# Building slot tables on one core: comparisons merged on VectorE, half of the bucket one-hots moved off GpSimd, slot one-hots scaled by GpSimd

## The reference, cut to what matters

```
h = relu(layernorm(x));  x = x + hypergraph_conv(relu(hypergraph_conv(h, W1, b1)), W2, b2)
    hypergraph_conv: xt = h @ W;  e = B_inv * segment_sum(xt[src], dst)
                     out = D_inv * segment_sum(e[dst], src) + b
h = relu(layernorm(x));  x = x + message_layer(h, src, dst, edge_weight)
    message_layer: e = silu(silu([h[src], h[dst], w] @ eW1 + eb1) @ eW2 + eb2)
                   agg = segment_sum(e, src);  out = silu([h, agg] @ nW1 + nb1) @ nW2 + nb2
```

## Time and profile before

| | us |
|---|---|
| median of 3 runs | 8857.22 (8846.52 to 8869.2) |
| profiled execution, its own time | 8864.02 |
| its span | 8862.3 |
| granted TensorE clock, mean | 0.956 |

### The profile page before, as it was taken

The page is one execution under the profiler, slowest core; times in us unless marked ns, Lnnn a source line. Parts: engine busy times, 40 slices in busy tenths (PEclk is TensorE's granted clock), DMA queues, the critical chain, the costliest instruction groups (busy, mean ns, idle before and its releaser), DMA issues. The chain is left out here.

```text
span 8862.3 us, 258190 instructions
## 1 busy us (share of the span) xinstructions
PE 7877.5 (89%) x80997; PEld 7191.2 (81%) x80997; DVE 7406.3 (84%) x20481; ACT 5157.5 (58%) x14322; POOL 2812.5 (32%) x4182
## 2 busy tenths in 40 slices
PE   2989998999989988999888899869999999999997
PEld 2777777777777778999788888759998999999995
DVE  7999999999999995777688888548888888888884
ACT  3777777777777770000577788425555555555553
POOL 4977778777777750000000000001111111111110
PEclk9999999999999999999799999759999999999998
DMA  2767667766676677666699999643333333333333
GB/s 71 158 152 157 154 153 157 155 155 153 156 156 153 156 159 199 190 191 170 148 223 222 214 245 245 139 142 109 104 106 106 103 106 106 105 104 105 107 104 74
DMA packets 1523049, 1310.03 MB, mean 148 GB/s; under 512 B 797344, under 2 KB 1337364, under 8 KB 1521212
## 3 DMA queue, kind: packets, MB, share of 16 engines
q1 hardware_dynamic: 1506126, 1269.86, 58.6%
q0 software_dynamic: 14112, 26.84, 1.2%
q10 hardware_dynamic: 1840, 0.53, 0.0%
HBM read 777.89 MB, written 361.62 MB: 129 GB/s over the span
## 5 line engine op out<-in xcount | busy, mean ns | idle before, releaser
L662 POOL TENSOR_SCALAR OH<-iot,kd 128x102 bf16<-128x102 bf16 x3440 | 2285.3, 683 | 3.5 <-PE S L799 3.5
L2257 POOL DMA_INDIRECT Qx<-tab_q,tidx x294 | 320.9, 1091 | 4904.5 <-DVE skt L2291 2584.5
L1478 PE MATMUL wp<-AF,XS 128*128 128x256 f32 x9604 | 1196.3, 283 | 167.6 <-issue 123.4
L841 PE MATMUL HP<-T3a,RB 128*128 128x193 bf16 x9604 | 1209.2, 249 | 124.3 <-ACT RB L965 124.3
L1478 PEld LDWEIGHTS wp<-AF,XS 128*128 128x128 f32 x9604 | 1148.5, 191 | 198.4 <-issue 198.3
L1504 ACT ACTIVATE AF<-RG 128x1536 fp32r<-128x1536 uint8 x686 | 1022.9, 1491 | 332.6 <-PE wp L1478 226.0
L965 ACT ACTIVATE RB<-PS 128x256 int16<-128x256 f32 x2401 | 895.6, 379 | 520.2 <-PE PS L826 479.2
L2278 ACT ACTIVATE Z<-Zb 128x512 f32<-128x512 f32 x882 | 556.1, 630 | 994.3 <-DVE Zb L2335 948.8
L841 PEld LDWEIGHTS HP<-T3a,RB 128*128 128x128 fp8e4 x9604 | 858.8, 98 | 249.1 <-issue 160.8
L926 ACT ACTIVATE LH<-LB,pl 128x64 f32<-128x64 bf16 (+8 forms) x4116 | 1008.4, 330 | 0.0
L2335 DVE TENSOR_TENSOR Zb<-p,eb2s 128x512 f32<-128x512 f32 x882 | 609.3, 691 | 450.1 <-PE p L2228 276.9
(11 more groups left out here) (344 smaller groups left out, 15460.4 us busy)
## 6 DMA issues: line engine op xcount, KB each, us to landing
RG<-adjT SPq DMA_DIRECT2D x1372, 224.0 KB, 6.6
sdb<-bk SPq DMA_DIRECT2D x245, 768.0 KB
adj<-RB SPq DMA_DIRECT2D x343, 448.0 KB, 2.8
adjT<-RT SPq DMA_DIRECT2D x686, 224.0 KB, 3.8
RG<-adj SPq DMA_DIRECT2D x686, 224.0 KB, 4.5
sdb<-bk SPq DMA_DIRECT2D x49, 384.0 KB
WR<-wk SPq DMA_DIRECT2D x882, 9.0 KB
tab_p<-Pst SPq DMA_DIRECT2D x25, 512.0 KB, 3.0
```

The lines of the kernel that those rows point to most:

```text
L662: ins = e.tensor_scalar(OH[:, g * GT + k, :], iot1[:, 0:KEYS], kd[:, g * GT + k:g * GT + k + 1], None, ALU.is_equal)
L841: ins = e.matmul(HP[:, h * W3:(h + 1) * W3], lhsT=pair[:, x_, h * P:(h + 1) * P], rhs=T3a[:, 2 * (u - 1) + x_, :], start=False, stop=True, ...
L1478: ins = e.matmul(ps[b][:, 0:256], lhsT=XS[:, n * PB + m, :, :].rearrange("p c f -> p (c f)"), rhs=AF[:, (b + n) % 3, m, :], start=n == 0 a ...
```

## The change

What it does:

1. **Counting.** The odd list is no longer packed as 256 * count. `OA` holds even and odd source one-hots of two units (512 elements, one instruction), `OB` is gone; `OD` of two units is one instruction of 1024 elements. TensorE writes even and odd counts side by side (512 columns), and ScalarE's `keep` reads 512 values and writes 512 bytes. `counted` is one instruction instead of five.
2. **Bucket one-hots.** VectorE makes those of the first `DT` = 3 tiles of a group in one instruction (`match`), three groups ahead; GpSimd makes the other two.
3. **Ranks.** VectorE adds neighbouring one-hots (`plus`, tile `SP`), and TensorE uses three matmuls of 306, 204 and 102 columns in place of four of 408, 306, 204 and 102.
4. **Slot one-hots.** VectorE compares all five tiles in one instruction (`LB`, 5 by the group's greatest width). ScalarE scales one tile (`AT` = 1), GpSimd the other four in one instruction (`scaled`).
5. GpSimd makes the next chunk's `kd` and `pl` at slot `KEY_AT` = 8 of the turn before, in two buffers.

```diff
-AT = 3
+AT = 1
+DT = 3
+AHEAD = 3
+KEY_AT = 8
...
 GpSimd
-                            for k in range(GT):
-                                ins = e.tensor_scalar(OH[:, g * GT + k, :], iot1[:, 0:KEYS], kd[:, g * GT + k:g * GT + k + 1], None, ALU.is_equal)
+                            for k in range(DT, GT):
+                                ins = e.tensor_scalar(OH[:, g * GT + k, :], iot1[:, 0:KEYS], kd[b][:, g * GT + k:g * GT + k + 1], None, ALU.is_equal)
                             ins.then_inc(v_oh, 1)
+                        def scaled(i, b, g):
+                            after(v_lb, i * NGR + (g + 1))
+                            after(p_s, i * NGR + (g - 1))
...
+                            e.tensor_tensor(LH[g % 2][:, AT:GT, :, 0:w], LB[g % 2][:, AT:GT, 0:w].unsqueeze(2).to_broadcast([P, n, 2, w]),
+                                            pl[b][:, :, t + AT:t + GT].rearrange("p c t -> p t c").unsqueeze(3).to_broadcast([P, n, 2, w]),
+                                            ALU.mult).then_inc(v_lh, 1)
...
 TensorE, ranks
+                            e.wait_ge(v_rk, added(v))
-                            for k in range(GT - 1):
-                                m = GT - 1 - k
-                                ins = e.matmul(b[:, (k + 1) * KEYS:GT * KEYS], lhsT=ones[:, :], rhs=w[:, k:k + 1, :].to_broadcast([P, m, KEYS]), ...
+                            e.matmul(tiles[:, 2:GT, :], lhsT=ones[:, :], rhs=SP[g % 2][:, 0:1, :].to_broadcast([P, GT - 2, KEYS]), ...
+                            e.matmul(tiles[:, 1:GT:2, :], lhsT=ones[:, :], rhs=w[:, 0:GT - 1:2, :], ...
+                            e.matmul(tiles[:, GT - 1, :], lhsT=ones[:, :], rhs=SP[g % 2][:, 1, :], ...
...
 ScalarE, keep
-                            e.activation(RB[n % NSLOT][:, k, :].bitcast(i16), bank(u)[:, 0:256], ACT.Copy,
-                                         accum_out=gs[:, u:u + 1]).then_inc(a_u, 1)
+                            e.activation(RB[n % NSLOT][:, k, :].bitcast(u8).rearrange("p (n x) -> p n x", x=2),
+                                         bank(u)[:, :].rearrange("p (x n) -> p n x", x=2), ACT.Copy, accum_out=gs[:, u:u + 1]).then_inc(a_u, 1)
...
 VectorE, ranks: behind the reductions now match(i, g + AHEAD, b) and plus(i, g + 2)
+                            e.tensor_tensor(OH[:, t:t + DT, :], iot1[:, 0:KEYS].unsqueeze(1).to_broadcast([P, DT, KEYS]),
+                                            kd[b][:, t:t + DT].unsqueeze(2).to_broadcast([P, DT, KEYS]), ALU.is_equal).then_inc(v_rk, 1)
+                            e.tensor_tensor(SP[g % 2][:, :, :], w[:, :, 0, :], w[:, :, 1, :], ALU.add).then_inc(v_rk, 1)
...
 VectorE, places
-                            for k in range(AT):
-                                ins = e.tensor_scalar(LB[g % 2][:, k, 0:w], by_rank(g, iot1, iotr, w), float(OWN - 1), rk[:, t:t + 1], ALU.add, ALU.is_equal)
-                            for k in range(AT, GT):
-                                ins = e.scalar_tensor_tensor(LH[g % 2][:, k, :, 0:w], ranked..., rk[:, t:t + 1], pl[:, :, t:t + 1]..., ALU.is_equal, ALU.mult)
+                            e.tensor_tensor(LB[g % 2][:, :, 0:w], by_rank(g, GT, w), rk[:, t:t + GT].unsqueeze(2).to_broadcast([P, GT, w]),
+                                            ALU.is_equal).then_inc(v_lb, 1)
...
 VectorE, unit
-                                for y in range(2 if u < NU - 1 else 1):
-                                    e.tensor_scalar(OB[k % PAIRS][:, y, :], iot1[:, 0:P], SBk[:, b:b + 1], 256.0, ALU.is_equal, ALU.mult)
+                                e.tensor_tensor(OA[k % PAIRS][:, 0:2 * n * P]..., (iot4 if n == 2 else iot2)[:, 0:P, :], SBs[:, b:b + 2 * n]..., ALU.is_equal)
+                                e.tensor_tensor(OD[k % PAIRS][:, 0:n, :, :], iot2..., SBd[:, b:b + 2 * n]..., ALU.is_equal).then_inc(v_un, 1)
```

More of the change, by code:

```diff
@@ L497, in gnn_kernel @@
                 LH = [sbt(p1, f"LH{n}", [P, GT, 2, P], fp32) for n in range(2)]
-                LB = [sbt(p1, f"LB{n}", [P, AT, P], bf16) for n in range(2)]
+                LB = [sbt(p1, f"LB{n}", [P, GT, P], bf16) for n in range(2)]
                 OHf = [sbt(p1, f"OHf{n}", [P, GT, KEYS], fp32) for n in range(2)]
@@ L519, in gnn_kernel @@
                 pl = [sbt(p1, f"pl{n}", [P, 2, TC], fp32) for n in range(2)]
-                kd = sbt(p1, "kd", [P, TC], fp32)
+                kd = [sbt(p1, f"kd{n}", [P, TC], fp32) for n in range(2)]
                 ddc = sbt(p1, "ddc", [P, 2], fp32)
@@ L525, in gnn_kernel @@
                 rj = sbt(p1, "rj", [P, KEYS], fp32)
+                SP = [sbt(p1, f"SP{n}", [P, 2, KEYS], bf16) for n in range(2)]
                 cb = [sbt(p1, f"cb{n}", [P, KEYS], bf16) for n in range(2)]
@@ L530, in gnn_kernel @@
                 room = sbt(p1, "room", [P, KEYS], bf16)
-                iotr = sbt(p1, "iotr", [P, P], bf16)
                 iofr = sbt(p1, "iofr", [P, P], fp32)
                 d_ct = sem("c_dct")
-                SBk = sbt(p1, "SBk", [P, 2 * KEYS], fp32)
+                SBk = sbt(p1, "SBk", [P, 4], fp32)
                 Ui = sbt(p1, "Ui", [P, P], bf16)
@@ L592, in wide_at, with seen, added, ranked @@
                     return WIDE[t % HT]
-                def by_rank(g, up, down, w):
-                    return up[:, 0:w] if g < HG else down[:, P - w:P]
+                def seen(v):
+                    return (3 * v - 2 if v >= AHEAD else v + 1) if isinstance(v, int) else v * 3 - 2
+                def added(v):
+                    return max(3 * v + 2, AHEAD + 1) if isinstance(v, int) else v * 3 + 2
+                def ranked(v):
+                    return v * 3 + (2 * AHEAD)
+                def used(t):
+                    w, g = wide_at(t), t // GT
+                    a = 0 if g < HG else wide_at(g * GT + GT - 1) - w
+                    return slice(a, a + w)
+                def by_rank(g, n, w):
+                    v = iofo[:, 0:w] if g < HG else iofr[:, P - w:P]
+                    return v.unsqueeze(1).to_broadcast([P, n, w])
                 def ends_of(v):
@@ L674, in turn @@
                         def turn(i, b, behind):
-                            keys(i)
-                            payload(i, b)
                             for g in range(NGR):
-                                onehots(i, g)
-                                if behind and g == NGR // 2:
-                                    diagonal(i - 2)
+                                if g == KEY_AT:
+                                    keys(i + 1, 1 - b)
+                                    payload(i + 1, 1 - b)
+                                onehots(i, b, g + AHEAD)
+                                scaled(i, b, g)
+                                if behind and g == NGR // 2:
+                                    diagonal(i - 1)
+                        keys(0, 0)
+                        payload(0, 0)
+                        for g in range(AHEAD):
+                            onehots(0, 0, g)
                         turn(0, 0, False)
-                        turn(1, 1, False)
+                        turn(1, 1, True)
                         turn(2, 0, True)
@@ L1080, in unit @@
                                 for q in range(4):
[L1081 to L1082 removed]
+                                    ins = e.tensor_scalar(OZ[:, q, :], iot1[:, :], SBk[:, q:q + 1], None, ALU.is_equal)
                                 ins.then_inc(v_un, 1)
@@ L1180, in _ @@
                         e.wait_ge(c_init, 4)
+                        for g in range(AHEAD):
+                            match(0, g, 0)
+                        plus(0, 0)
+                        plus(0, 1)
                         turn(0, 0, True, False, False, False)
```

138 lines of the change are left out of this document (68 added, 70 removed).

## The result

| | before | after |
|---|---|---|
| median, us | 8856.67 (8846.52 to 8869.2, 4 runs) | 8644.92 (8638.71 to 8657.88, 4 runs) |
| span of the profiled execution | 8862.3 | 8637.0 |
| granted TensorE clock, mean | 0.956 | 0.96 |

The ratio is 0.9762, 95% interval 0.9745 to 0.9779: 2.4% faster. 8675 was predicted, 8460 to 8900 as the range.

A forecast was written before the change was run, and what follows sets the result against it. VectorE was taken to bound building: 51.7 us of work, 2.3 of gaps and 7.0 of port stalls make 61.0 a turn against 64.7. Over 48 turns, plus 5 us for turn 0, that gives 8675 us; range 8460 to 8900.

The forecast's parts named there:

- VectorE bounds the turn: Building: VectorE's instructions set the turn, 62.4 us of work in 64.7, falling to 51.7 of work with the change.
- The merged instructions' rates: VectorE in building: units 23.3 us a turn instead of 31.6, places save 9.0, match adds 5.7, plus adds 2.7.
- The port: Building: GpSimd's products and VectorE's two-tensor instructions exclude each other in SBUF, stalling VectorE 7.0 us a turn.
- the bounds of 2.8 and 12.2: VectorE's stall a turn: 2.8 us if products start during PSUM reads, 12.2 if they always get in between unit instructions.
- The gaps: VectorE's time between instructions in a building turn, 2.3 us, kept unchanged and added to 51.7 for 54.0 us.
- The other engines stay below: Building, per turn: TensorE below 56.1 us, ScalarE 47.8, GpSimd 35.8 before any stall, so none was forecast to bind.
- the change touches building alone: Premise that only the building stage changes, so only its turns were forecast and no gain in the message stage.
- Rival 1: Building: the port costs little and TensorE becomes the bound; turns of 55 to 58 us, 8400 to 8540; chance 0.25.
- Rival 2: Building: stalls past 10.7 us, or slow `keep`, undo the change; turn about 66 us, 8926, or 9200 by `keep`; chance 0.15.
- Rival 3: Building: no effect, stalls of 10 to 11 us give back what merging saves; 8830 to 8880 us; chance 0.08.
- -8.3 -1.8: VectorE's forecast savings a building turn from counting: 8.3 us on units, 1.8 on counted and sorted_.
- -9.0 +5.7 +2.7 +7.0: VectorE's forecast terms a building turn: places save 9.0 us; match adds 5.7, plus 2.7, stalls by GpSimd's products 7.0.

The follow-up runs named there:

- e_vscale: Against the changed kernel: VectorE scales the four tiles itself, in one instruction behind LB, and GpSimd does no product; 8544 us, ratio to before 0.983, turn 63.14 us.
- c_rest: The changed kernel with its counting part undone, so parts 2 to 5 of the change alone; 9003 us, ratio to before 1.020, turn 70.54 us.
- e_split: The changed kernel with each GpSimd product of four tiles split into two products of two tiles; 8469 us, ratio to before 0.976, turn 61.55 us.
- e_at2: The changed kernel with AT = 2: ScalarE scales two tiles of a group, GpSimd three; 8474 us, ratio to before 0.974, turn 61.43 us.
- l_after_msg: The changed kernel with 117 more TensorE semaphore increments, putting the message loop where it stands in the kernel before; 8586 us, ratio to before 0.988.
- b_count_at2: The kernel before with the counting part alone, AT = 2 and 139 more TensorE semaphore increments ahead of the message stage; 8389 us, ratio 0.951, turn 58.11 us.
- c_count: The kernel before with the counting part of the change alone; 8538 us, ratio to before 0.984, turn 61.38 us.

## Why the prediction was right, and where not

The total of 8675 is 30 us off, and that it is so close is luck: 183 us were predicted for building and 103 came; 118 came from the message stage, for which the prediction had nothing. The two errors cancel. What was right without luck is the direction, the bound and most terms of the turn; building alone would have given about 8763, still within the range.

- *VectorE bounds the turn, and still does.* Right: 60.2 of 62.75 us busy.
- *The merged instructions' rates.* Right. By the almost undisturbed means of e_vscale less 0.08 us: units 25 x (0.61 + 0.35) = 24.0 us (23.3 predicted), match 14 x 0.40 = 5.6 (5.7), plus 14 x 0.18 = 2.5 (2.7). VectorE's work without stalls is 52.3 us, 51.7 predicted.
- *The port.* The mechanism is shown (e_vscale). The term was too small: 7.0 predicted, 7.9 of standing still measured, and c_rest (7.7), e_split (6.6) and e_at2 (5.3, with three tiles) are between the bounds of 2.8 and 12.2 as well. That the one value chosen between them, 7.0, came this near is partly chance. What was left out is where the stalls fall: small steps of about 0.2 us take 1.34 (`cinv_d`), 1.29 (`E`) and 0.79 us (`w`) when a product meets them.
- *The gaps.* 2.3 us were carried over from before; after, 62.75 - 60.2 = 2.5. With 0.6 of work, 0.9 of stall and 0.2 of gaps, the turn comes to 62.7.
- *The other engines stay below.* Right: ScalarE 47.0 us (47.8), `keep` 601 ns (620). TensorE is busy 56.5, below 62.75. GpSimd has 43.5 us; 35.8 were predicted before any stall.
- *The step that failed* is the one before all others: "the change touches building alone". It touches building's text alone. Parts 2 to 5 moved everything behind them on TensorE by 117 instructions, and the loop of the message stage lost its gaps. Without that the first comparison would be 8645 + 118 = about 8763, 1.1% faster and not 2.4%. That is a working from the stage's length, and l_after_msg bears it out with 0.988 on chip A, where the stage's difference is 49 us; on chip B it is 60.
- *Rival 1* (the port costs little) fell with e_vscale. *Rival 2's* outcome, slower, is that of parts 2 to 5 taken alone (c_rest, 1.020), but not by its mechanism: the stalls there are 7.7 us, not over 10.7. The counting part paid for it. *Rival 3* (stalls give back just what the merging saves) holds of GpSimd's products by themselves: they bring VectorE 9.8 us and cost 9.4.

The prediction also didn't take the change apart. The sum "-8.3 -1.8" for counting and "-9.0 +5.7 +2.7 +7.0" for the rest stood in it: by it the rest was a loss of 6.4 us for VectorE. The only thing for it was ScalarE's relief, which one tile on VectorE gives more cheaply (b_count_at2).

## What to carry to other kernels

Add the terms up for each part of a change by itself; a part that is a loss can hide behind one that is a gain, and a helper engine can cost the engine that it helps nearly all that it takes off it (9.4 of 9.8 us here). When a stage that nobody edited changes its time, look for `issue` gaps in the middle of one statement inside a loop, and move the loop by some hundred instructions (117 and 139 did it here) before believing any other cause. Compare two versions of a long program stage by stage, or with later loops at the same place.

## What the runs showed of the hardware

- Products on GpSimd stop VectorE whole: a two-element copy took 1342 ns and ended with the product. The Trainium skill, SBUF — State Buffer, section Who interferes with whom, calls the shared pair an exclusive lock held for the whole instruction, and Perfetto Trace Analysis, section Optimizing Scalar/DVE Operations, warns that moving work between the two might not help. The trace agrees, with a balance of 0.35 us a turn.
- It goes the other way as well: GpSimd's one-hots, which have a scalar and one streamed tensor, have means of 687, 765 and 789 ns in before, c_count and b_count_at2, and 852 in e_vscale, where VectorE does the products as well, with a minimum of 525 to 530. So GpSimd waits as well when VectorE has much two-tensor work; no run changes that alone.
- Loop position on TensorE: at one place of the loop 1.4 to 2.2 us of nothing in each pass of two pairs (about 104 us), 49 to 120 us in all, the same when moved by 256 instructions; at the other place none.
